# A one-layer perceiver kernel: first group's queries and keys in two token parts, other load order, layer norm in 10 steps, new instruction orders

## The chip, the core and the metric

One core of a Trainium2 chip runs the whole layer. TensorE (PE) multiplies and transposes, VectorE (DVE), ScalarE (ACT) and GpSimd (POOL) do the elementwise work, and the queues of SyncE (SP) and ScalarE issue the DMAs. The metric is the device time of one execution in microseconds; the value of a kernel is the median of its runs.

## The reference, cut to what matters

The input is `x`, 64 batches of 32 rows of 256 channels, and a context of 257 rows of 192 channels for each batch. All tensors are float32.

```
x = x + xattn(ln(x), ctx)   # 16 heads of 64; keys, values from the 257 context rows; mask; softmax
x = x + attn(ln(x))         # 16 heads of 16 over the batch's own 32 rows
x = x + ffn(ln(x))          # r * (relu(k)^2 @ W_v), x mixed with its previous row by mu_r, mu_k
ln(x) = (x - mean) / sqrt(var + 1e-5)
```

Each of the first two blocks applies a second layer norm with its own gamma and beta, so one fused scale serves both norms of a block.

## The kernel before, in words

**Tiling.** The 64 batches go in 8 groups of 8 batches (`GB = 8`), a group being 256 token rows (two tiles of 128). Three stages of different groups run at once: the pre stage of group g+1 (norm, transposed input `xnT`, queries `qT`, and keys folded into the queries), the attention of the 8 batches of group g, and the post stage of group g-1 (output product, second attention, gated layer). Keys are never formed: a query times its key weights (`nwk`, `nwkt`) gives a 192 wide row for each head and query, and that row is multiplied with the raw context. Each such number is held as an upper and a lower part of the reduced float type, `qk_h` and `qk_l` for channels 0 to 127 and `qk_t` for both parts of channels 128 to 191. ACT copies the upper part out of PSUM, DVE subtracts it from PSUM for the lower one.

**Jobs and orders.** Every engine but SP runs a list of named jobs, written out by hand for the first, the middle and the last group (`PE_FIRST`, `PE_ORDER`, `PE_LAST` and the same for ACT, DVE and POOL). An engine runs its jobs strictly in that order; semaphores hold a job until what it needs is done. The names, with j the batch in the group:

- `CT:j` transposes the context of batch j on PE (L724), copies it (ACT L1043) and splits it (DVE L1290). `CU:j` and `CL:j` make the upper and lower parts of the untransposed context (ACT L1077, DVE L421 and L422). After `CL:j` nothing reads the loaded buffer `cx_in` of that batch again.
- `S0:j` to `S3:j`: scores of four heads each, five products (PE L780), mask and maximum (DVE L1299), exponent (ACT L1051). `R` is the reciprocal, `N` the normalisation (POOL L564).
- `P0:j`, `P1:j`: transposed probabilities (PE L791, ACT L1059), `U` and `L` their parts (ACT L1070, POOL L430). `AC:j`: probabilities times context (PE L806 to L812), copied by ACT L1083, L1084 and DVE L1312.
- `XT`, `Q0` to `Q3`: transposed norm and queries. `K0` to `K11`: the twelve halves of the six key products (PE L701 and L710, issued by the even ones; ACT L1029 and L1034, DVE L1276 and L1281). In the first group the same jobs are called `H0` to `H11`, and `Q2`, `Q3` are `G2`, `G3`.
- `A`, `B`, `C` followed by a number: one step each of the three layer norms (DVE L1235 to L1258). A step waits for the step before it.
- `LV0`, `LV1`: value product of the last context row of all 64 batches (PE L744, L745, ACT L1175). `F0` to `F2` transpose the gated layer's weights. `OT`, `WO`, `T2`, `QT`, `KT`, `VR`, `SC`, `PT`, `PV`, `T4`, `PJ`, `T3`, `FR`, `FK`, `FV`: post stage. `LT` spreads the last row's probabilities. `Z` is a filler product on PE (L945).
- In the last group the post stage runs in two halves of 128 rows, `.0` and `.1`.

**Start.** PE runs 36 warm-up products (`WARM`), the input transposes, the eight weight transposes of the keys (`WK0` to `WK3`, L984, L985), the last context rows, and queries `Q0` and `Q1` for all 256 rows, each query product being 4 pairs of 256 columns. Only then the list `PE_FIRST` begins.

**SP's queue.** SP issues the loads in program order: input, key weights, first half of the query weights, context 0, second half, contexts 1 to 3, the rest. Then, for group 0, it waits for the copies of `LV0` and `LV1`, issues 16 small DMAs that spread the last row's values (`spread_last_values`, L499), and only then enters the loop over the batches: wait until `AC:j` is done (`ac_done`), load the context of batch j+4 into the same slot (L451, L453). There are four slots.

Of the kernel before, what the change touches and what calls it, by code (L numbers as in the profile page):

```python
# [12 lines left out]
ALU = mybir.AluOpType  # L13
ACT = mybir.ActivationFunctionType
AX = mybir.AxisListType
# [23 lines left out]
RSQRT_SEED = float(0x5F3759DF)  # L39
NEWTON = 3  # L40
# [5 lines left out]
FIRST_USE_0 = {0: 4, 1: 6, 2: 10, 3: 12}  # L46
# [21 lines left out]
    "AC:5 P1:6 K4 P0:7 K6 AC:6 LT P1:7 K8 K10 CT:0 AC:7").split()  # L68
PE_ORDER = (
# [3 lines left out]
    "S1:7 S2:7 FR P0:6 S3:7 FK AC:5 FV P1:6 K0 K2 AC:6 P0:7 K4 LT P1:7 K6 CT:0 K8 K10 AC:7").split()  # L73
PE_LAST = (
# [5 lines left out]
    "T3.1 Z16 FR.0 FK.0 FR.1 FK.1 Z17 Z18 FV.0 Z19 FV.1").split()  # L80
ACT_FIRST = (
# [4 lines left out]
    "U0:6 K3 P1:6 K4 U1:6 AC:5 K5 K6 CU:7 P0:7 K7 AC:6 U0:7 P1:7 K8 U1:7 K9 CT:0 K10 K11 AC:7").split()  # L86
ACT_ORDER = (
# [4 lines left out]
    "AC:5 P1:6 U1:6 K0 K1 K2 K3 AC:6 P0:7 K4 U0:7 K5 K6 K7 P1:7 CT:0 U1:7 K8 K9 K10 K11 AC:7").split()  # L92
ACT_LAST = (
# [5 lines left out]
    "T3.0 M0.0 T3.1 M0.1 FK.0 EZ.0 FK.1 EZ.1").split()  # L99
# [1410 lines left out]
```

## Time and profile before

| | |
|---|---|
| median of 3 runs | 874.78 us (873.36 to 875.11) |
| profiled execution | 873.3 us |
| its span, first to last instruction | 870.3 us |
| mean granted TensorE clock | 0.988 |
| PE busy | 812.6 us, 93% |
| DVE, ACT, POOL busy | 611.1, 600.3, 423.7 us |
| 16 DMA engines, queue of SP | 12.3% of the span |

The profiled execution took 3.0 us more than its span. The granted clock is a mean of two levels: 1.0 is 2.4 GHz, 0.5 is 1.2 GHz. In the 40 slices of the page PE stands at 98 to 99% nearly everywhere in the middle (digits of 9, and 8 at the borders of the groups), and lower in the first five slices, which are 109 us, and in the last five.

### The profile page before, as it was taken

The page shows a single profiled execution, that of the slowest core. Times are in us where ns is not written, and L with a number is a line of the kernel's source. Part 1 is how long each engine was busy: PE and PEld are TensorE (multiplying, and loading weights), DVE is VectorE, ACT ScalarE, POOL GpSimd, SP SyncE. Part 2 cuts the span into 40 slices and gives each one's busy share as a digit, 9 for nine tenths or more (in the row PEclk, how much of TensorE's full clock was granted, in tenths as well). Part 3 has the DMA queues.
Part 4 walks back from the last instruction along what each step waited for, and adds up shares of the span by engine and source line. Part 5 has one row for each costly group of instructions (what it writes and reads, how often), then busy time and mean ns, then how long its engine had stood idle before and what let it go on. Part 6 is the DMA issues. An engine that isn't in the chain of part 4 may idle for free.

```text
span 870.3 us, 20253 instructions
## 1 busy us (share of the span) xinstructions
PE 812.6 (93%) x7355; PEld 669.2 (77%) x7355; DVE 611.1 (70%) x1871; ACT 600.3 (69%) x1423; POOL 423.7 (49%) x664
## 2 busy tenths in 40 slices
PE   8779999999999989999999989999999989888886
PEld 7568669896788858896788868896788857677664
DVE  4744575879577884879567884879668874767375
ACT  2659876798477875799567975799567875667422
POOL 1155524665437534766337533766337534656211
PEclk9899999999999999999999999999999999999999
DMA  8311010010101020011101120110100110010000
GB/s 236 109 25 37 26 50 13 25 26 26 50 26 26 25 62 13 26 27 25 50 18 29 29 62 14 26 26 25 50 14 26 36 51 10 17 26 1 26 2 12
DMA packets 49521, 30.50 MB, mean 35 GB/s; under 512 B 22928, under 2 KB 48336, under 8 KB 49424
## 3 DMA queue, kind: packets, MB, share of 16 engines
q1 hardware_dynamic: 48528, 29.12, 12.3%
q8 instruction: 59, 0.97, 0.4%
q14 instruction: 38, 0.31, 0.1%
q10 hardware_dynamic: 896, 0.10, 0.1%
HBM read 26.85 MB, written 2.10 MB: 33 GB/s over the span
## 4 chain that ended last, share of the span: by engine, by line
PE 74%; DVE 12%; ACT 8%; issue 4%; SPq 1%; POOL 1%; DMA 0%; POOLq 0%; ACTq 0%; DVEq 0%
PE score L780 16%; PE pre L665 6%; PE post L866 6%; PE probT L791 5%; DVE qk_t L1281 4%; PE post L875 3%; PE aux L724 3%; PE ac_main L806 3%; PE ac_tail L808 2%; PE ac_main L807 2%; PE ac_tail L812 2%; PE ac_main L811 2%; DVE qk_l L1276 2%; PE post L846 2%; PE post L884 2%
## 5 line engine op out<-in xcount | busy, mean ns | idle before, releaser
L430 POOL TENSOR_TENSOR prT_l<-prT,prT_h 128x512 fp32r<-128x512 f32 x128 | 164.5, 1290 | 173.0 <-ACT prT_h L1070 172.8
L564 POOL TENSOR_SCALAR pr<-pr,rsum,poison 128x257 f32<-128x257 f32 x256 | 148.8, 593 | 138.0 <-DVE rsum L1305 137.0
L1299 DVE CUSTOM_DVE_ANT_0 sm<-score,mbias 128x257 f32<-128x257 f32 x256 | 106.5, 420 | 92.6 <-PE score L780 78.8
L1051 ACT ACTIVATE pr<-sm,nmx 128x257 f32<-128x257 f32 x256 | 128.8, 505 | 42.9 <-DVE nmx L1299 37.5
L780 PE MATMUL score<-cT_h,qk_h 128*128 128x258 f32 x256 | 91.6, 358 | 6.2 <-DVE qk_t L1281 4.7
L1059 ACT ACTIVATE prT<-probT 128x512 f32<-128x512 f32 x128 | 75.6, 591 | 30.0 <-PE probT L791 28.2
L791 PE MATMUL probT<-ident,pr 128*128 128x128 f32 x512 | 78.8, 277 | 9.3 <-ACT prT L1059 7.0
L1070 ACT ACTIVATE prT_h<-prT 128x512 fp32r<-128x512 f32 x128 | 80.2, 627 | 8.2 <-PE ac_tail L812 7.4
L791 PEld LDWEIGHTS probT<-ident,pr 128*128 128x128 f32 x512 | 60.3, 142 | 19.5 <-issue 7.1
L780 PE MATMUL score<-cT_h,qk_t 128*128 128x258 f32 x256 | 73.7, 288 | 0.0
L780 PE MATMUL score<-cT_h,qk_l 128*128 128x258 f32 x256 | 73.4, 287 | 0.0
L780 PE MATMUL score<-cT_l,qk_h 128*128 128x258 f32 x256 | 73.3, 286 | 0.0
L780 PE MATMUL score<-cT_l,qk_t 128*128 128x258 f32 x256 | 73.1, 286 | 0.0
L780 PEld LDWEIGHTS score<-cT_h,qk_h 128*128 128x128 f32 x256 | 49.3, 192 | 17.7 <-DVE qk_t L1281 7.6
L1083 ACT ACTIVATE act_low<-ac_tail 64x512 f32<-64x512 f32 x64 | 38.1, 595 | 35.3 <-PE ac_tail L812 33.7
L1290 DVE TENSOR_TENSOR cT_l<-aux,cT_h 128x512 fp32r<-128x512 f32 x64 | 43.5, 679 | 24.8 <-ACT cT_h L1043 24.0
L1312 DVE TENSOR_TENSOR act_<-ac_tail,act_low 64x256 f32<-64x256 f32 x128 | 52.9, 413 | 7.9 <-ACT act_low L1083 6.7
L806 PE MATMUL ac_main<-prT_h,c_hl 128*128 128x512 f32 x128 | 55.2, 431 | 2.8 <-ACT prT_h L1070 2.2
L665 PE MATMUL pre<-xnT,wq 128*128 128x256 f32 x232 | 55.6, 382 | 0.0
L780 PEld LDWEIGHTS score<-cT_l,qk_h 128*128 128x128 f32 x256 | 49.7, 194 | 1.4
L866 PE MATMUL post<-wo,qT 128*128 128x256 f32 x224 | 50.6, 379 | 0.0
L808 PE MATMUL ac_tail<-prT_h,c_hl 128*128 128x512 f32 x128 | 50.3, 393 | 0.0
(336 smaller groups left out, 2195.6 us busy)
## 6 DMA issues: line engine op xcount, KB each, us to landing
cx_in<-in_ctx_dram SPq DMA_DIRECT2D x64, 192.0 KB, 2.4
cx_in<-in_ctx_dram SPq DMA_DIRECT2D x64, 64.0 KB, 2.3
xn<-in_x_dram SPq DMA_DIRECT2D x8, 256.0 KB, 3.2
xb<-in_x_dram SPq DMA_DIRECT2D x8, 256.0 KB, 3.3
out_dram<-yo SPq DMA_DIRECT2D x7, 256.0 KB, 3.0
wq<-in_L_xattn_Wq_dram SPq DMA_DIRECT2D x2, 512.0 KB, 7.8
wo<-in_L_xattn_Wo_dram SPq DMA_DIRECT2D x1, 1024.0 KB, 8.2
wqkv<-in_L_attn_W_qkv_dram SPq DMA_DIRECT2D x1, 768.0 KB, 8.7
```

What stands on the lines that cost most here:

```text
L430: eng.tensor_tensor(prT_l[:, :, cut], prT[:, :, cut], prT_h[:, :, cut], ALU.subtract).then_inc(prob_lower, 1)
L564: last = pool.tensor_scalar(p, p, rsum[:, j % 2, t:t + 1], poison[:, 0:1], ALU.mult, ALU.mult)
L665: last = pe.matmul(bank[:, i * TOK:(i + 1) * TOK], wq[:, k, (2 * n + i) * P:(2 * n + i + 1) * P], xnT[:, k, :], start=(k == 0), stop=(k == 1))
L780: last = pe.matmul(score[t % 2][:, 0:NK + 1], q[:, j, tile], c, start=(i == 0), stop=(i == len(products) - 1))
L791: last = pe.transpose(probT[:, m * 256 + i * P:m * 256 + (i + 1) * P], pr[j % 2][:, 2 * half + i, m * P:(m + 1) * P], ident[:])
L806: pe.matmul(ac_main[:], c[:, m, UPPER], prT_h[:, m, :], start=(m == 0), stop=False)
L808: pe.matmul(ac_tail[:], c[:, m, TAILS], prT_h[:, m, :], start=(m == 0), stop=False)
L866: last = pe.matmul(bank[:, 0:DM], qT[:, k, w * P:(w + 1) * P], wo[:, k, :], start=(k == 0), stop=(k == NPAIR - 1))
L1051: act.activation(pr[j % 2][:, t, :], sm[:, t % 2, :], ACT.Exp, bias=nmx[:, j % 2, t:t + 1], scale=-1.0, accum_out=ssum[:, j % 2, t:t + 1]) ...
L1059: act.activation(prT[:, :, half * 256:(half + 1) * 256], probT[:].rearrange("p (m c) -> p m c", m=2), ACT.Copy).then_inc(probT_copied, 1)
L1070: act.activation(prT_h[:, :, cut], prT[:, :, cut], ACT.Copy).then_inc(prob_upper, 1)
L1299: dve.tensor_tensor_reduce(sm[:, t % 2, :], score[t % 2][:, 0:NK], mbias[:], DH ** -0.5, BIG, ALU.add, ALU.min, nmx[:, j % 2, t:t + 1]).th ...
```

## The change

The edits are these.

1. **First group in two token parts.** The queries of group 0 are computed as `D0`, `D1` (rows 0 to 127, that is batches 0 to 3; heads 0 to 7, then 8 to 15) and `G0`, `G1` (rows 128 to 255). Each is 8 products of 128 columns. The keys become `H0` to `H5` for the first part and `I0` to `I5` for the second, each pair of them covering two of the six key products at 128 columns. Copies and splits follow, with half as many columns. The scores of batch 0 now wait for `H` alone (`S0` for two of six, `S1` for four, the rest for six), those of batch 4 for `I`.
2. **Query weights are loaded ahead of the key weights** on SP's queue, and the start of PE is `WARM`, `XT`, then the list, which begins with fillers `O` and `D0`; the key weights' transposes are `J0` to `J3` in the list. Last rows (`LF`), constants (`CN`) and context 0 (`T0`) are list jobs as well.
3. **Context loads** wait for `c_lower` (the split `CL:j`) where they waited for `ac_done` (the product `AC:j`). The 16 small DMAs move from ahead of the batch loop to behind the load that batch 1 triggers.
4. **Layer norm** has 10 steps (16 instructions for 256 rows) where it had 12 (19): one step makes the seed of the reciprocal root, and two refinements with other constants take the place of three.
5. **New orders** for all four engines and all three lists. `Z` has 19 fillers where it had 20.

```diff
 sp.dma_start(xn[:], token_rows(x_rows, 0)).then_inc(x_in, 16)
+sp.dma_start(wq[:, :, 0:512], wq_columns[:, :, 0:512]).then_inc(wq_in, 16)
 sp.dma_start(wk_main, Wkv[0:P, 0:NH * DH]).then_inc(wk_staged, 16)
 sp.dma_start(wk_tail, Wkv[P:DC, 0:NH * DH]).then_inc(wk_staged, 16)
-sp.dma_start(wq[:, :, 0:512], wq_columns[:, :, 0:512]).then_inc(wq_in, 16)
 load_ctx(0, 0)
...
-                else:
-                    spread_last_values()
                 for j in range(GB if has_pre else GB - NCTX):
-                    sp.wait_ge(ac_done, g * GB + j + 1)
+                    sp.wait_ge(c_lower, g * GB + j + 1)
                     load_ctx(g * GB + j + NCTX, j % NCTX)
+                    if g == 0 and j == 1:
+                        spread_last_values()
...
+            def first_queries(name):
+                half, tokens = int(name[1]), slice(0, TP) if name[0] == "D" else slice(TP, TOK)
...
+                pe.wait_ge(pre_free, nth_pre({"G0": "D0", "G1": "G0"}.get(name, "XT"), 0))
+                for i in range(4):
+                    pair = 4 * half + i
+                    for k in range(2):
+                        last = pe.matmul(FIRST_PRE_BANKS[name][:, i * TP:(i + 1) * TP], wq[:, k, pair * P:(pair + 1) * P],
+                                         xnT[:, k, tokens], start=(k == 0), stop=(k == 1))
...
                 elif stage == 2:
                     dve.tensor_scalar(w[:, own], mv[:, n, own, 1], -0.5 * scale, -0.5 * shift, ALU.mult, ALU.add)
-                    last = dve.tensor_scalar(lw[:, n, 3, own], mv[:, n, own, 1], scale, shift, ALU.mult, ALU.add)
+                    last = dve.tensor_scalar(w2[:, own], mv[:, n, own, 1], -1.6875 * scale, -1.6875 * shift, ALU.mult, ALU.add)
                 elif stage == 3:
-                    last = dve.tensor_scalar(li[:, n, own], lw[:, n, 3, own].bitcast(I32), 1, None, ALU.logical_shift_right)
-                elif stage == 4:
-                    last = dve.tensor_scalar(y[:, own].bitcast(I32), li[:, n, own], -1.0, RSQRT_SEED, ALU.mult, ALU.add)
+                    last = dve.tensor_scalar(y[:, own].bitcast(I32), w[:, own].bitcast(I32), -0.5, RSQRT_SEED, ALU.mult, ALU.add)
```

The new list of PE for the first group, up to the fourth batch, and the tail of a middle group before and after:

```
PE_FIRST  O0 O1 O2 O3 O4 O5 D0 J0 O6 J1 J2 H0 J3 LF T0 D1 G0 H2 H4 CT:1 O7 O8 O9 S0:0 S1:0 I0 G1 S2:0 S3:0 I2
          S0:1 CT:2 S1:1 P0:0 S2:1 S3:1 I4 P1:0 S0:2 S1:2 P0:1 CT:3 S2:2 S3:2 AC:0 P1:1 S0:3 S1:3 CT:4 S2:3 LV0
          P0:2 S3:3 LV1 P1:2 S0:4 F0 AC:1 P0:3 S1:4 F1 CT:5 S2:4 S3:4 XT F2 AC:2 P1:3 S0:5 S1:5 Q0 S2:5 P0:4 CT:6
before    K0 K2 AC:6 P0:7 K4 LT P1:7 K6 CT:0 K8 K10 AC:7 | S0:0 CT:1 S1:0 OT0 S2:0 S3:0 OT1
after     K0 K2 P0:7 AC:6 K4 K6 P1:7 LT K8 AC:7 CT:0 K10 | S0:0 CT:1 S1:0 OT0 CT:2 S2:0 S3:0 OT1
```

In DVE's last list the steps `C0.0` to `C8.0` stand ahead of `PJ.1` now (before: `C0.0` to `C2.0`), and `C9.0`, the step that writes the normed half, stands behind `C2.1`. `FV.0` moves ahead of `SG.1`.

## Rows read from the trace of the kernel before

**Rows 1.** Windows: stretch, length, busy PE, PEld, DVE, ACT, POOL, clock, DMA.

```profile
8.42:118.86 110.44, 94.43 (x651) 75.04 (x650) 60.49 (x190) 78.41 (x181) 43.21 (x77) 0.94 0.26 74
...
30.00:35.50 5.50, 2.05 (x25) 1.26 (x21) 4.29 (x12) 4.96 (x11) 1.11 (x3) 0.89 0.00 0
35.50:43.00 7.50, 7.46 (x32) 6.20 (x32) 5.02 (x19) 3.48 (x10) 1.33 (x4) 0.62 0.01 3
...
68.00:98.00 30.00, 29.23 (x191) 26.44 (x190) 13.66 (x54) 26.85 (x66) 17.86 (x27) 1.00 0.14 36
98.00:117.40 19.40, 16.20 (x147) 10.70 (x146) 14.64 (x32) 17.40 (x35) 10.48 (x17) 1.00 0.11 28
117.40:711.00 593.60, 579.13 (x5341) 480.86 (x5341) 451.55 (x1372) 444.23 (x1049) 317.32 (x486) 1.00 0.11 30
```

**Rows 2.** PE's waits, 120 to 720 us: total, times, longest.

```profile
PE score L710 <- DVE qk_l L1276: 4.3, 6, 0.7
...
PE probT L791 <- ACT prT L1059: 2.7, 6, 0.5
```

**Rows 3.** Timeline, 47 to 62 us: SP's queue and the PE transpose behind it.

```profile
49.44 9.08 SPq L499 DMA_DIRECT2D lvc<-kM  x14
...
58.56 0.44 SPq L451 DMA_DIRECT2D cx_in<-in_ctx_dram  x1
...
61.49 0.97 PE L724 MATMUL aux<-ident,cx_in 128*128 128x128 f32 x4 [4.88 <-DMA cx_in<-in_ctx_dram]
```

**Rows 4.** Timeline of PE: first scores of batch 4 and of group 1.

```profile
68.25 0.36 PE L780 MATMUL score<-cT_h,qk_h 128*128 128x258 f32 x1 [0.20 <-issue]
...
118.86 0.36 PE L780 MATMUL score<-cT_h,qk_h 128*128 128x258 f32 x1 [0.78 <-DVE qk_t L1281]
```

**Rows 5.** The chain that ended last: start, duration, what.

```profile
1.53 6.89 PE score L989 x36
...
21.02 1.02 PE score L701 x16
...
65.76 0.23 PE ac_main L806
...
75.21 1.73 PE pre L665 x8
76.94 0.44 PE probT L791 x4
...
84.92 0.60 PE score L780 x5
...
820.60 0.60 PE score L852 x16
...
825.15 0.89 PE post L875 x8
```

**Rows 6.** ACT and DVE by shape: busy us, mean ns, idle before.

```profile
L1121 ACT ACTIVATE qT<-score 128x256 f32<-128x256 f32 x2 | 0.7, 381 | 2.6 <-PE score L858 2.6
...
L1029 ACT ACTIVATE qk_h<-score 128x512 fp32r<-128x512 f32 x30 | 17.1, 595 | 1.1 <-PE score L701 1.1
...
L1312 DVE TENSOR_TENSOR act_<-ac_tail,act_low 64x256 f32<-64x256 f32 x128 | 52.9, 413 | 7.9 <-ACT act_low L1083 6.7
```

**Rows 7.** The page: DMA issues; KB each, median us to landing.

```profile
wq<-in_L_xattn_Wq_dram SPq DMA_DIRECT2D x2, 512.0 KB, 7.8
```

**Rows 8.** Timeline, 311 to 316 us, around a group's border.

```profile
311.54 2.41 ACT L1034 ACTIVATE qk_t<-score 64x512 fp32r<-64x512 f32 x4
...
312.91 2.81 DVE L1281 TENSOR_TENSOR qk_t<-score,qk_t 64x512 fp32r<-64x512 f32 x4
...
315.78 0.39 PE L780 MATMUL score<-cT_h,qk_h 128*128 128x258 f32 x1 [0.65 <-DVE qk_t L1281]
```

**Rows 9.** Timeline of the end, 851 to 856 us.

```profile
851.95 0.42 DVE L1390 TENSOR_TENSOR x<-ac_tail,xb 128x256 f32<-128x256 f32 x1 [3.38 <-PE ac_tail L915]
...
855.51 0.41 PE L637 MATMUL pre<-ident,hn 128*128 128x128 f32 x2 [2.73 <-DVE hn L1249]
```

More of the change, by code:

```diff
@@ L336, in nth, with nth_pre @@
             return g * len(jobs) + list(jobs).index(name) + 1
+        def nth_pre(name, g):
+            if g == 0:
+                return PRE_FIRST.index(name) + 1
+            return len(PRE_FIRST) + nth(PRE, name, g - 1)
         def stream(orders):
@@ new lines, in key_products @@
+                last = [None, None]
+                for i in range(2):
+                    for e in range(2):
+                        cols = slice(place + i * n_tok, place + (i + 1) * n_tok)
+                        for c in range(2):
+                            rows, cut = slice(e * 64, e * 64 + 64), slice(c * 64, c * 64 + 64)
+                            if kind == "main":
+                                pair, weight = 2 * at + i, nwk[rows, 2 * at + i, cut]
+                            else:
+                                pair, weight = 4 * at + 2 * i + c, nwkt[rows, 4 * at + 2 * i + c, :]
+                            last[e] = pe.matmul(banks[e][cut, cols], weight, qT[rows, pair, tokens], start=True, stop=True)
@@ new lines, in key_products, with first_key_job @@
+                return last
+            def first_key_job(name):
+                n, later = int(name[1:]), name[0] == "I"
+                if n % 2:
+                    return
+                job = n // 2
+                pe.wait_ge(pre_free, nth_pre(f"{'DG'[later]}{min(job, 1)}", 0))
+                if name == "H0":
+                    pe.wait_ge(setup_copied, 2)
+                if name == "H2":
+                    pe.wait_ge(setup_copied, 4)
+                    pe.wait_ge(left_split, 1)
+                if name in ("H4", "I0"):
+                    pe.wait_ge(qk_split, 2 if name == "H4" else 4)
+                if name in ("I2", "I4"):
+                    pe.wait_ge(qk_split, 6 if name == "I2" else 10)
+                banks = FIRST_QK_BANKS[later * len(FIRST_QK) + job]
+                for x, d in enumerate(FIRST_QK[job]):
+                    last = key_products(d, banks, slice(TP, TOK) if later else slice(0, TP), x * TOK, TP)
+                for e in range(2):
+                    last[e].then_inc(qk_full, 1)
@@ L941, in post_job, with key_weights, last_rows, warm @@
                 last.then_inc(post_full, 1)
+            def key_weights(n):
+                if n == 0:
+                    pe.wait_ge(wk_staged, 32)
+                if n == 3:
+                    pe.wait_ge(setup_copied, 1)
+                for i in range(2):
+                    pair = slice((2 * n + i) * P, (2 * n + i + 1) * P)
+                    pe.transpose(wk_bank[n][:, i * DC:i * DC + P], wk_main[:, pair], ident[:])
+                    last = pe.transpose(wk_bank[n][:, i * DC + P:(i + 1) * DC], wk_tail[:, pair], ident[0:64, 0:64])
+                last.then_inc(keys_full, 1)
+            def last_rows():
+                pe.wait_ge(left_staged, 32)
+                pe.wait_ge(setup_copied, 2)
+                pe.transpose(left_bank[:, 0:NB], left_in[:, 0:P], ident[0:NB, 0:NB])
+                pe.transpose(left_bank[:, NB:2 * NB], left_in[:, P:256], ident[0:NB, 0:NB]).then_inc(left_full, 1)
+            def warm():
+                pe.matmul(warm_bank[:, 0:P], ident[:], ident[:], start=True, stop=True)
             def keep_clock():
@@ L1019, in pre_job, with first_queries @@
                 last.then_inc(pre_free, 1)
+            def first_queries(name):
+                act.wait_ge(pre_full, nth_pre(name, 0))
+                half, tokens = int(name[1]), slice(0, TP) if name[0] == "D" else slice(TP, TOK)
+                act.activation(qT[:, 4 * half:4 * half + 4, tokens], FIRST_PRE_BANKS[name][:].rearrange("p (n t) -> p n t", n=4),
+                               ACT.Copy).then_inc(pre_free, 1)
             def qk_copy(n, g):
@@ L1156, in post_job, with last_rows @@
                 last.then_inc(post_copied["ScalarE"], 1)
+            def last_rows():
+                act.wait_ge(left_full, 1)
+                rows_in = left_bank[:, 0:2 * NB]
+                by_group = rows_in.rearrange("p (k g b) -> p k g b", k=2, g=NG)
+                act.wait_ge(zeroed, 1)
+                act.activation(left[:, 0].rearrange("p (b g) -> p g b", g=NG), by_group[:, 0], ACT.Copy)
+                for r in range(2):
+                    rows = slice(r * 64, r * 64 + 64)
+                    act.activation(left[rows, 1 + r].rearrange("p (b g) -> p g b", g=NG), by_group[rows, 1], ACT.Copy)
+                act.activation(left_h[:].rearrange("p k b -> p (k b)"), rows_in, ACT.Copy).then_inc(left_upper, 1)
             def run():
                 for name, g, j in stream(ACT_STREAM):
-                    if name[0] == "H":
-                        qk_copy(int(name[1:]), 0)
-                    elif name in ("G2", "G3"):
-                        pre_job("Q" + name[1], 0)
+                    if name in KEYS_FIRST:
+                        first_key_copy(name)
+                    elif name in PRE_FIRST and g == 0 and name != "XT":
+                        first_queries(name)
+                    elif name == "T0":
+                        context(0, "CT0", 0)
+                    elif name == "LF":
+                        last_rows()
                     elif name == "CT":
@@ L1227, in layer_norm @@
                 before = 0 if half == 1 else g * LN_LINKS
-                w, y, q = lw[:, n, 0], lw[:, n, 1], lw[:, n, 2]
+                w, y, q, w2 = (lw[:, n, i] for i in range(4))
                 if stage > 0:
@@ L1271, in qk_lower, with first_key_lower @@
                 d, e = divmod(n, 2)
+                key_lower(d, e, qk_banks[d % 2][e][:], slice(0, GB)).then_inc(qk_split, 1)
+            def first_key_lower(name):
+                n, later = int(name[1:]), name[0] == "I"
+                dve.wait_ge(qk_upper, later * N_FIRST_QK + n + 1)
+                job, e = divmod(n, 2)
+                bank = FIRST_QK_BANKS[later * len(FIRST_QK) + job][e]
+                for x, d in enumerate(FIRST_QK[job]):
+                    last = key_lower(d, e, bank[:, x * TOK:(x + 1) * TOK], slice(HB, GB) if later else slice(0, HB))
+                last.then_inc(qk_split, 1)
```

300 lines of the change are left out of this document (138 added, 162 removed), and 78 rows, old and new, of tables (ACT_FIRST, ACT_LAST, ACT_ORDER, DVE_FIRST).

## The prediction

> **What bounds the kernel now.** I began with the page's shares and its 40 slices: PE is busy 93% of the span, no other engine over 70%, and PE's clock is at its upper level almost throughout. So the end is set by PE's work and by the gaps in it, and the question for every edit is which gap of PE it closes. The windows show where the gaps are [rows 1]. From 117.4 to 711 us PE is busy 579.13 of 593.60 us at clock 1.00; the 14.5 us of idle there are four waits in each of six group borders, 14.0 us in all and 2.33 us a group; the largest (4.3 us) and the smallest (2.7) of the four stand in [rows 2]. In the opening, from the end of the warm-up to the first score of group 1, 8.42 to 118.86 us, PE is busy 94.43 of 110.44 us at clock 0.94: 16.0 us idle, and since a clock of 0.94 is the mean of 1.0 and 0.5, 0.06 x 110.44 = 6.6 us more lost to work at 1.2 GHz. With neither, the same work is 110.4 - 16.0 - 6.6 = 87.8 us. Third, the waits and the timeline name the largest single gap: PE stands 4.88 us before the context transpose of batch 4, because its load stands in SP's queue behind the 16 small DMAs, fourteen of which take 9.08 us [rows 3]. Another gap is 30 to 35.5 us, where PE is busy 2.05 of 5.5 us, waiting for copies and splits of keys, and behind it the clock is 0.62 for 7.5 us, which costs 0.38 x 7.5 = 2.9 us [rows 1].
>
> **Context loads and the 16 DMAs.** The load for batch 4 now waits for the split of batch 0's context, which stands ahead of batch 0's second score on DVE, and the small DMAs are behind the load for batch 5. The 4.88 us go. What is late next is batch 6's load: it stands behind the 16 DMAs, and these behind the copy of `LV1`. They take 16 x 9.08 / 14 = 10.4 us, copy and landing add 0.6 and 61.49 - 58.56 = 2.9 us, so batch 6 is there 13.9 us after `LV1`'s product. In that time PE has, by the list up to `CT:6`, 7 score tiles, 8 jobs of four transposes (P, XT, CT:5, F0 to F2), 1 query job and 2 of `AC`: 7 x 0.60 + 8 x 0.44 + 1.73 + 2 x 10 x 0.23 = 14.1 us [rows 5]. It is covered with 0.2 us to spare; if that cover fails it costs what is missing, and at most the 4.88 us of before. In later groups no context wait is among the four, so the earlier loads give nothing there.
>
> **Query weights first.** Both 512 KB halves take about 7.8 us to land [rows 7], the first issued at 2.4 us. The three transfers that change places carry the same bytes, so the last of the three lands near 10 us in either order. `D0` needs the query weights and the copies of `XT`, which run to 10.0 us; the key weights are needed at 11.9, behind `D0`. Neither waits for the load. The input transposes cannot start before the warm-up ends at 8.42 [rows 5], so the 0.6 us that the shorter first norm gives is hidden there: nothing.
>
> **Two token parts, and the new opening.** The columns are the same, the instructions twice as many. A query job of 128 columns costs between 8 x 0.111 us by the post row of 128 columns (825.15 us, 0.89 for 8) and its share by columns, 1.73 / 16 = 0.108: 64 of them are 6.9 to 7.1 us for 6.9 before. For keys the nearest row is the 64x64 product of 128 columns, 16 in 0.60 us, 37.5 ns each; 192 of them are 7.2 us for 6 x 1.02 = 6.1 before [rows 5]. So PE gains 1.1 to 1.3 us of work; the bounds are 0 (columns alone) and 6.1 (an instruction costs as at 256 columns); I take 1.3. ACT and DVE pay too: half the columns cost 0.38 for 0.60 us, and a 64x256 operation 0.41 [rows 6]; twelve copies of 8 x 0.60 + 8 x 0.60 = 9.6 us become 16 x 0.38 + 16 x 0.38 = 12.2 at worst and, as neighbouring ones overlap, some 1.5 us more than before. DVE likewise gains 2.5. What it buys is the order of things. Walked by the new list with these prices, PE gets `D0` 10.1 to 11.9, the key weights and `H0` to 17.1, `D1`, `G0`, `H2`, `H4` to 23.1, the first score at 24.2; `I0` and `G1` lie between scores; `AC:0` runs 39.4 to 41.7, and batch 4's first score, with both `LV` done, comes at 49.3. In the trace that score is at 68.25 [rows 4], with `AC:1` and `XT` done as well (2.7 us) and `P1:2` not (0.44): like for like 66.0 against 49.3, 16.7 us.
>
> That walk has every engine ready at once. Two things say not to take it whole. ACT: it has 78.4 us of work in the stretch and gets 1.5 more, so in a stretch of 94 us it would be busy 85%, and between 68 and 98 us it already runs at 26.85 of 30 [rows 1]; its list is what holds `AC:0`, `P0:1` and the keys `I`. And the 3.2 us of idle in 98 to 117.4 us come from the key jobs at the group's end, which keep their form. So I give 87.8 + 1.3 + 8.4 of gaps = 97.5 us for the stretch, 12.9 less. The 8.4 is 3.2 for the end, 2.0 for `D0`'s wait and the fillers `O7` to `O9`, and 3.2 that ACT or a short low clock takes. Bounds: 17 by the walk, 5 if only batch 4's wait goes.
>
> The Trainium skill speaks against this part. Its page "TensorE: Matmul & The Clock Gate", section "Back-to-back issue gap", says that a stream of weight load and product pairs runs at about 81 ns a product at 128 columns and not at the column time. By it 192 key products would be 15.6 us, 9.5 more than now, and the gain would be 4 us. The trace has the same form, 64x64 with 128 columns, at 37.5 ns, four in flight on different quarters of the array [rows 5]; so I go by the row.
>
> **Layer norm.** Three instructions of 19 go for 256 rows. In the middle DVE is busy 451.55 of 593.60 us, and its norm steps fill gaps between PE's scores: nothing. In the end it counts: the second projected half's sum starts at 851.95 and PE waits 2.73 us until the first half's norm is written and transposed at 855.51 [rows 9]. With steps `C0.0` to `C8.0` ahead of that sum, in a time in which DVE is idle 3.38 us, the first half needs only the sum, three short steps and the write behind it: 0.42 + 0.45 + 0.2 + 0.2 + 0.4 = 1.8 us, so the transpose comes at 853.8, 1.7 earlier. The second half is 1.0 earlier, two steps of 0.2 and less interleaving. `FV.0` ahead of `SG.1` is neutral: the last store hangs on `FV.1`. I take 1.5 from this and 0.5 from the second half's earlier norm, two steps shorter with PE behind it: 2.0, bounds 0 and 4.
>
> **Orders of the middle groups.** Here the gain or loss is six times a small number. The new tail puts `CT:0` and `AC:7` between `K8` and `K10`. Before, `S0:0` waits 0.65 us for the second key split of `K8`/`K9`, ACT's four copies of 2.41 us and DVE's four of 2.81 starting 1.2 and 2.6 us after `K8` [rows 8]. After, PE has 10 x 0.23 + 0.44 + 1.02 = 3.8 us from `K8`'s end to `S0:0`, 0.44 more cover, but the copy of `CT:0` stands behind the four on ACT and its split of 0.69 behind them on DVE, which makes `S0:0` ready 0.7 us later. `K8` itself has lost `CT:0` as cover and ACT's `U0:7` ahead of it. Counting from `K0` to `S0:0` I get 15.1 us in both orders. The other two waits keep their form. I take 0, bounds -7 (half of the 14.0 gone) and +6 (1 us a group). The last group's reordering, 4 us around it either way by its own idle, I take at 0.
>
> **Sum.** The profiled execution: 873.3 - 12.9 - 2.0 = 858.4. The median of the runs is 874.78, 1.5 above it, so 858.4 to 859.9: I say 859.
>
> **The rivals.**
> - *ACT bounds the opening.* For it: 26.85 of 30 us busy in 68 to 98 us. Against: 80 us of work in 97.5. If it must run its whole list at 89.5% behind its idle until 15.6 us (the first key copy): 80 - 4 = 76 us of work at 0.895 is 85 us, to 100.6, and the key tail adds 8 us more than PE's floor: the gain is 6 to 8, time 866.
> - *The orders help the middle.* For it: all 14.0 us are the same four waits. Against: my count. Half of them gone: 852.
> - *The block of 16 DMAs only moves.* If `CT:6` waits as `CT:4` did, 4.88 us, and the clock stays: 864. Against: 14.1 us of PE work over 13.9.
> - *A product of 128 columns costs as one of 256.* Against: 37.5 and 111 ns beside 64 and 216 [rows 5], in this very program. For it: those rows are 24 products in the calm end. Keys would cost 6.1 us more than before and queries 6.9, 13.0 in place of 1.3: 871. The page on TensorE named above has keys dearer still.
> - *Slower: group borders.* `S0:0` waits for `CT:0`'s split, last in a queue of four key splits. Priced above at +0.7 against +0.44 of cover. If more stood ahead of it, each border would lose; the gain of 15 is used up at 15 / 7 = 2.1 us a border, seven of them. And after 3.45 us of idle in 5.5 the clock was low long enough to cost 2.9 [rows 1]: 2.1 + 2.9 a border make 859 + 35 = 894; without the clock 874 to 876. The page "TensorE: Matmul & The Clock Gate" of the Trainium skill, section "HAM oscillation — how this bites in real kernels", has gaps bring the clock down each time, with half of the work's speed as the price.
>
> **How the numbers follow.** Forecast 0.61 at 859 (own range 854 to 864), ACT 0.15 at 866, orders 0.10 at 852, the 16 DMAs 0.06 at 864, products at 256 columns' price 0.02 at 871, slower border 0.06 at 876 and up. A measurement of this kernel can tell 0.2%, 1.7 us, from no change. The first five cases are faster, 0.94 together; from them I take 0.01 for what I have not seen. Of the last case, with that, 0.05 is slower and 0.02 the same: 0.93, 0.02, 0.05. The range from 850 to 868 takes in the first four with their own spread.
>
> **What would show it.** Right: `CT:4` without a DMA wait, and that load issued near 25 us; the first score of batch 4 near 50 to 53 us, of group 1 near 106; clock 0.98 or more from 8.4 to 106; 192 key products of the first group under 45 ns apart; 99 us a group as before; the `T3.0` transpose 1.5 us or more nearer to `PJ.1`'s sum. Wrong: key or query products at 80 ns; a border wait over 2 us; ACT without a gap from 40 to 100 us and PE waiting for it; a wait before `CT:6`.

## The result and the profile after

The changed kernel takes 844.56 us (median of 4 runs, 844.47 to 844.77), the kernel before beside it 874.94 us (873.36 to 876.49): a ratio of 0.966, 95% interval 0.9641 to 0.9679. It is 30.4 us faster. The forecast was 859 us with a range of 850 to 868: the direction was right, the gain half of what came, and the time is outside the range.

The first score of each group divides the span (profiled executions, us; "a group" is the mean of the six periods of groups 1 to 6):

| kernel | first score | from it to group 1's | a group | last group | span | execution |
|---|---|---|---|---|---|---|
| before | 28.25 | 90.61 | 98.60 | 159.87 | 870.3 | 873.3 |
| after | 23.75 | 75.76 | 98.46 | 152.44 | 842.7 | 844.6 |
| forecast, against before | -4 | -9 | 0 | -2 | -15 | |
| measured | -4.5 | -14.9 | -0.1 each, -0.8 | -7.4 | -27.6 | -28.7 |

The last 1.1 us lie outside the span (3.0 before, 1.9 after).

Now the page and the windows of the kernel after (stretch, length, busy PE, PEld, DVE, ACT, POOL, clock, DMA), which answer to [rows 1]:

```profile
PE 799.9 (95%) x7501; PEld 665.1 (79%) x7501; DVE 600.3 (71%) x1813; ACT 604.0 (72%) x1439; POOL 415.0 (49%) x664
PEclk9999999999999999999999999999999999999999
```

```profile
8.42:99.51 91.09, 88.65 (x795) 75.20 (x795) 64.02 (x203) 77.64 (x196) 43.44 (x77) 1.00 0.34 96
50.00:70.00 20.00, 20.00 (x135) 18.30 (x134) 10.87 (x39) 18.38 (x48) 12.37 (x20) 1.00 0.22 54
70.00:90.00 20.00, 19.26 (x155) 15.28 (x154) 12.18 (x33) 18.51 (x44) 13.04 (x24) 1.00 0.11 27
90.00:99.51 9.51, 7.95 (x61) 5.92 (x62) 9.09 (x19) 8.36 (x16) 4.11 (x5) 1.00 0.31 84
99.51:690.26 590.75, 575.85 (x5339) 477.81 (x5338) 440.60 (x1316) 446.78 (x1045) 310.68 (x484) 1.00 0.11 30
690.26:842.70 152.44, 128.55 (x1331) 105.18 (x1329) 92.37 (x280) 78.12 (x197) 58.07 (x89) 1.00 0.05 13
```

From 8.42 us to the first score of group 1 PE is busy 88.65 of 91.09 us, where before it was 94.43 of 110.44 at clock 0.94. The clock never falls there. And ACT is busy 36.89 of the 40 us from 50 to 90, 92%, while PE is busy 39.26 of them: a full ACT beside a full PE. PE's waits of that stretch (total, times, longest; the first is the wait at the very start) are all that is left of its idle time, 1.2 + 0.6 + 0.6 = 2.4 us:

```profile
PE score L993 <- POOL ident L532: 1.5, 1, 1.5
PE ac_main L835 <- DVE act_ L1387: 1.2, 1, 1.2
PE score L712 <- DVE qk_l L1352: 0.6, 1, 0.6
PE pre L712 <- DVE qk_t L1356: 0.6, 1, 0.6
```

SP's timeline answers to [rows 3], and PE's to [rows 4] and [rows 5]: the load for batch 4 is issued at 24.57 us and its transposes start at 43.05 with no wait; the 16 DMAs take 10.62 us behind batch 5's load; the first keys' products, which the program places on four quarters of the array, overlap.

```profile
24.57 0.38 SPq L452 DMA_DIRECT2D cx_in<-in_ctx_dram  x1
46.67 0.37 SPq L452 DMA_DIRECT2D cx_in<-in_ctx_dram  x1
49.87 10.62 SPq L500 DMA_DIRECT2D lvc<-kM  x16
60.53 0.45 SPq L452 DMA_DIRECT2D cx_in<-in_ctx_dram  x1
```

```profile
9.68 2.02 PE L673 MATMUL probT<-xnT,wq 128*128 128x128 f32 x16
14.79 0.28 PE L712 MATMUL pre<-qT,nwk 64*64 64x128 f32 x2
14.90 0.28 PE L712 MATMUL pre<-qT,nwk 64*64 64x128 f32 x2
43.05 0.60 PE L746 MATMUL aux<-ident,cx_in 128*128 128x128 f32 x4
49.56 0.37 PE L807 MATMUL score<-cT_h,qk_h 128*128 128x258 f32 x1
99.51 0.28 PE L807 MATMUL score<-cT_h,qk_h 128*128 128x258 f32 x1
```

In 0.11 us between two such rows PE issues four key products, two of `pre` and two of `post`: 27 ns each. With the step from one job to the next the 192 key products of the first group take 6.05 us, 31 ns each; before, 96 of twice the columns took 6.1. In the last group the output projection's first product and, at the end, the two rows that answer to [rows 9]:

```profile
786.71 3.69 PE L895 MATMUL pre<-wo,qT 128*128 128x256 f32 x16 [0.17 <-ACT qT L1179]
827.23 0.42 DVE L1465 TENSOR_TENSOR x<-ac_tail,xb 128x256 f32<-128x256 f32 x1 [3.56 <-PE ac_tail L944]
829.05 0.41 PE L638 MATMUL pre<-ident,hn 128*128 128x128 f32 x2 [0.99 <-DVE hn L1308]
```

From the second half's sum to the first half's transpose it is 1.82 us, against 3.56 before. Behind it stand four products for each half, `FR.0` and `FR.1`. The same program ("after again" below) had them at the other clock level in a second execution; first the kernel after, then that one:

```profile
831.40 1.10 PE L961 MATMUL post<-wrT,kM 128*128 128x256 f32 x4 [0.34 <-DVE kM L1479]
```

```profile
831.10 2.04 PE L961 MATMUL post<-wrT,kM 128*128 128x256 f32 x4 [0.34 <-DVE kM L1479]
```

From `FR.0` to `FR.1` it is 1.83 us in the first, 3.29 in the second and 3.05 in the kernel before. So 1.2 us of the last group's 7.4 are an execution in which the clock stayed up, and not the change.

### The profile page after: what moved, and what is told of

Its sections match the earlier page's. It is cut to its first block, busy times and chain, and to the rows that moved or that the text cites. A ratio compares the mean times of both kernels' runs of the same rounds, so it can differ in the third digit from the quotient of the medians.

```text
span 842.7 us, 20502 instructions
## 1 busy us (share of the span) xinstructions
PE 799.9 (95%) x7501; PEld 665.1 (79%) x7501; DVE 600.3 (71%) x1813; ACT 604.0 (72%) x1439; POOL 415.0 (49%) x664
## 4 chain that ended last, share of the span: by engine, by line
PE 78%; DVE 14%; ACT 3%; issue 3%; POOL 1%; POOLq 0%; ACTq 0%; DVEq 0%
PE score L807 17%; PE probT L818 6%; PE post L895 6%; PE pre L657 6%; DVE qk_t L1356 4%; DVE qk_l L1352 3%; PE post L904 3%; PE aux L746 3%; PE ac_main L835 3%; PE ac_tail L837 3%; PE ac_main L836 3%; PE ac_tail L841 3%; PE ac_main L840 2%; PE post L875 2%; PE post L881 2%
## 5 line engine op out<-in xcount | busy, mean ns | idle before, releaser
L565 POOL TENSOR_SCALAR pr<-pr,rsum,poison 128x257 f32<-128x257 f32 x256 | 146.3, 582 | 131.2 <-DVE rsum L1380 131.1
L818 PEld LDWEIGHTS probT<-ident,pr 128*128 128x128 f32 x512 | 58.5, 141 | 16.3 <-issue 12.2
L835 PE MATMUL ac_main<-prT_h,c_hl 128*128 128x512 f32 x128 | 55.5, 434 | 4.2 <-ACT prT_h L1128 3.0
L657 PE MATMUL pre<-xnT,wq 128*128 128x256 f32 x224 | 52.9, 379 | 0.0
L1101 ACT ACTIVATE cT_h<-aux 128x512 fp32r<-128x512 f32 x64 | 37.8, 590 | 17.8 <-PE aux L746 13.4
L836 PE MATMUL ac_main<-prT_h,c_hl 128*128 128x512 f32 x128 | 50.1, 392 | 0.0
```

The costliest lines, as they stand in the source:

```text
L565: last = pool.tensor_scalar(p, p, rsum[:, j % 2, t:t + 1], poison[:, 0:1], ALU.mult, ALU.mult)
L657: last = pe.matmul(pre[:, i * TOK:(i + 1) * TOK], wq[:, k, (2 * n + i) * P:(2 * n + i + 1) * P], xnT[:, k, :], start=(k == 0), stop=(k == 1))
L818: last = pe.transpose(probT[:, m * 256 + i * P:m * 256 + (i + 1) * P], pr[j % 2][:, 2 * half + i, m * P:(m + 1) * P], ident[:])
L835: pe.matmul(ac_main[:], c[:, m, UPPER], prT_h[:, m, :], start=(m == 0), stop=False)
```

## The experiments

Fifteen other kernels ran, and the kernel after again. The last column is the median of the kernel before on the same chip (single runs of it 869.2 to 875.8 us, the longer ones with a lower mean clock, 0.984 to 0.994); the split by first scores tells more than the medians:

| kernel | first score | to group 1's | a group | last group | median us | before beside it |
|---|---|---|---|---|---|---|
| b_sp | 29.48 | 88.22 | 98.58 | 160.1 | 869.3 | 871.7 |
| b_rest | 29.05 | 90.78 | 98.45 | 154.06 | 865.9 | 871.7 |
| b_ln10 | 28.00 | 90.49 | 98.93 | 158.25 | 873.7 | 872.7 |
| after again | 23.50 | 75.75 | 98.45 | 153.97 | 845.5 | 873.9 |
| a_acdone | 23.43 | 84.12 | 98.46 | 152.52 | 852.2 | 871.7 |
| a_spread0 | 24.45 | 86.93 | 98.45 | 154.22 | 858.0 | 871.7 |
| a_wkfirst | 24.55 | 75.78 | 98.43 | 152.49 | 845.0 | 872.7 |
| a_nofill | 23.57 | 76.24 | 98.46 | 152.55 | 844.6 | 873.9 |
| a_actload | 23.42 | 76.80 | 98.41 | 152.44 | 846.1 | 873.9 |
| a_oldorder | 24.42 | 75.77 | 98.56 | 154.63 | 846.7 | 871.3 |
| a_oldlast | 23.68 | 75.81 | 98.36 | 159.67 | 851.2 | 871.3 |
| a_cbehind | 24.02 | 75.77 | 98.44 | 155.27 | 847.6 | 871.3 |
| a_ln12 | 24.07 | 75.82 | 99.24 | 158.65 | 855.9 | 871.3 |
| a_openonly | 24.05 | 75.80 | 98.58 | 158.88 | 852.7 | 872.7 |
| a_v1 | 24.19 | 75.77 | 98.43 | 151.84 | 844.3 | 873.9 |
| a_v2 | 23.44 | 75.80 | 98.43 | 150.76 | 843.1 | 872.7 |

The first score varies by 1.0 us between kernels with one opening, with the start of XT's transposes (7.42 to 8.50 us), for which PE waits on the norm or is still at the warm-up; from there to the first score it is 15.9 to 16.0 us in all of them. The last group varies by 1.5 us between two executions of one kernel ("after again" against after), by whether the clock falls in the last 20 us. The other two columns repeat to 0.1 us between these two. A name with a is an edit of the kernel after, with b of the kernel before.

**The context loads alone (b_sp).**

```
-                else:
-                    spread_last_values()
                 for j in range(GB if has_pre else GB - NCTX):
...
-                    sp.wait_ge(ac_done, g * GB + j + 1)
+                    sp.wait_ge(c_lower, g * GB + j + 1)
                     load_ctx(g * GB + j + NCTX, j % NCTX)
+                    if g == 0 and j == 1:
+                        spread_last_values()
```

> The kernel before with the context loads' change alone: SyncE waits for the copies (c_lower) and the 16 copies of last rows stand behind batch 1's load. Theory (TensorE is starved in the opening by whatever it waits for, and ScalarE does not hold it): TensorE's 4.88 us wait for batch 4's context goes, and with it the lower clock behind it; first score of group 1 from 118.86 to 112 to 114 us, the time 868 to 870 us against 874.9. Rival (ScalarE bounds the opening, so what TensorE gains it waits off again at ScalarE): at most 2.5 us, 872.4 or more. Second rival (the block of 16 only moves and holds batch 6): the same, with a wait of TensorE for a context load near 70 us.

The ratio is 0.9984 (0.9963 to 1.0005): it cannot be told from no change. The median lies in the theory's 868 to 870 us, but the kernel before took 871.7 beside it and not 874.9, and the first score of group 1 came at 117.70 us and not at 112 to 114: the theory failed. The stretch got 2.4 us shorter, though the DMA's 4.9 us of wait are gone. PE's waits from 28 to 118 us:

```profile
PE probT L791 <- ACT prT L1059: 3.0, 3, 1.2
PE ac_main L806 <- DVE act_ L1312: 1.9, 1, 1.9
PE post L701 <- DVE qk_l L1276: 1.9, 1, 1.9
PE probT L791 <- POOL pr L564: 1.6, 1, 1.6
PE post L701 <- DVE qk_t L1281: 0.9, 1, 0.9
```

No DMA is among them. Before, the first was 2.5 us and the second was not there; the last stands there too, just ahead of 28 us. So 4.9 us went and 2.4 came: in the old opening another chain stood right behind the DMA's. The rival's size, 2.5 us at most, is right. That ScalarE alone sets it is not shown: 0.5 us of the new wait are its own, but 1.9 are for a VectorE step, which stands in VectorE's list behind one that had waited 2.06 us for an exponent of ScalarE. The clock from 50 to 70 us was 0.91, as before.

**Parts of that edit taken back in the new opening (a_acdone, a_spread0).**

```
 a_acdone
-                    sp.wait_ge(c_lower, g * GB + j + 1)
+                    sp.wait_ge(ac_done if g == 0 else c_lower, g * GB + j + 1)
 a_spread0
-                    if g == 0 and j == 1:
+                    if g == 0 and j == 0:
```

> The kernel after, but the context loads of the first group wait for the products with the probabilities (ac_done) again; the 16 copies stay behind batch 1's load. Theory (in this opening every stall of TensorE counts in full): context 4 lands near 44.9 where its transposes want it at 43.05, context 5 is late by another 1, context 6 behind the 16 copies by 2, context 7 by 1 to 2: plus 4 to 7 us, 849 to 852. Rival (the slack of the opening takes the stalls up): plus at most 2 us.

> The kernel after with the 16 copies of last rows ahead of context 5's load, not behind it. Theory: they are issued from 49.9 to 60.5 us, context 5 lands near 63.8 and TensorE wanted it at 54.47: a stall of 9.3 us, with the lower clock behind it 9 to 11 us in all: 854 to 856. Rival (later slack takes part of it back): plus 5 us or less.

The stretch grows by 8.4 and 11.2 us. PE's waits for context loads, of a_acdone and then of a_spread0, and then two windows, of a_acdone behind its waits and of a_spread0 around the stall:

```profile
PE aux L746 <- DMA cx_in<-in_ctx_dram: 6.1, 4, 2.2
```

```profile
PE aux L746 <- DMA cx_in<-in_ctx_dram: 8.7, 1, 8.7
```

```profile
70.00:90.00 20.00, 18.80 (x113) 16.33 (x115) 7.62 (x30) 15.83 (x42) 9.39 (x16) 0.92 0.11 29
```

```profile
50.00:70.00 20.00, 11.30 (x63) 10.43 (x63) 4.76 (x20) 9.03 (x23) 6.38 (x13) 0.74 0.16 40
```

Each costs its stall and 2.3 or 2.5 us on top, and the clock, 1.00 there in the kernel after, is 0.92 and 0.74 in these windows: part of the work ran at the lower of the two levels. Slack takes nothing back, and both cost a little more than their theories said (4 to 7 and 9 to 11 us). The edits are not the same as b_sp's: b_sp makes both changes, in every group, and gains 2.4 us in the old opening, while a_acdone takes back only the one, in the first group, and loses 8.4 in the new one. So the smaller part is worth more in the new opening than both in the old, and the two parts of the opening cannot be priced apart and added.

**Everything but the opening (b_rest), and the opening alone (a_openonly).** b_rest has the lists `*_FIRST`, the one-part queries and keys, and the loads of group 0 of the kernel before, with the norm and the other lists of the kernel after; a_openonly the reverse.

> The kernel after with the opening of the kernel before (its first-group orders, all tokens in one part, key weights loaded first, 16 copies first, loads of the first group behind ac_done), but with the new layer norm and the new orders of groups 1 to 7. Theory: the opening is worth 19.35 us by itself and the rest 8 to 9: first score of group 1 near 118.5, end behind the first score of group 7 near 152.5 us, the time 863 to 866 us. Rival (the opening's gain comes partly from the new middle orders or the norm): first score of group 1 below 117 us.

> The kernel after with its opening alone: orders of groups 1 to 7 and the norm of 12 steps as in the kernel before. Theory (norm and orders pay only together; the old orders have room for 12 steps): first score of group 1 as in the kernel after, 75.8 us behind the first score, six periods of 98.6, the last group 159.9: 852.5 to 854.0 us, that is faster than the norm of 12 steps in the new orders (855.9). Rival (the two are independent: the norm costs 11 us wherever it stands, the old orders 8): 860 or more.

Both hold: 90.78 us to group 1, as before's 90.61, with all else new, and 75.80 with all else old. The opening is worth 20.1 us of the 28 to 30 (852.7 against 872.7), the rest 5.8 by b_rest's medians (865.9 against 871.7), less than the 8 to 9 expected; in b_rest's trace the clock fell at the end as in "after again", which is 1.5 us of it.

**Does ACT bound the opening (a_actload)?** Behind each half's upper parts of batches 2 to 7:

```
+                        if g == 0 and j >= 2:
...
+                            act.activation(yo[:]...[:, slot:slot + P], ident[:], ACT.Copy)
```

> The kernel after with twelve more ScalarE copies of 128x128 in the opening (one behind each half's upper parts of batches 2 to 7, into a tile that is free then), 3.3 to 3.7 us of ScalarE's time. ScalarE was busy 36.89 of the 40 us from 50 to 90. Theory (TensorE's queue sets this opening and ScalarE has slack behind each product): first score of group 1 later by 1.5 us at most. Rival (ScalarE bounds the opening): later by 3 us or more.

The twelve copies of 0.30 us, 3.6 us, cost 1.05 us, under the theory's 1.5. ACT now runs 37.86 of the 40 us from 50 to 90, 95%, and PE still 39.21:

```profile
50.00:70.00 20.00, 19.76 (x132) 17.89 (x131) 10.87 (x39) 18.78 (x52) 11.97 (x20) 1.00 0.22 54
70.00:90.00 20.00, 19.45 (x156) 15.40 (x154) 11.70 (x32) 19.08 (x47) 13.14 (x24) 1.00 0.11 27
```

**Fillers (a_nofill) and the weights' place (a_wkfirst).** The first drops `O0` to `O9` from `PE_FIRST`; the second issues the two key-weight loads ahead of `wq`.

> The kernel after without the ten fillers O0 to O9 on TensorE in the opening. Theory (they stand in waits and keep the clock up; the waits themselves do not change): minus 0.2 to plus 0.3 us if the clock stays at its higher level without them, plus 1 to 3 us in the stretch to the first score of batch 0 if it does not. Rival (they cost what they take, 10 products of 128 columns at 0.22 us): minus 1 to minus 2 us.

> The kernel after with the key weights' two loads issued ahead of the first query weights'. Theory (D0 starts at 9.68 us when the norm's transposes are copied; the query weights behind the key weights landed at about 9 to 10 us in the kernel before): first score later by 0 to 0.7 us, the time within 1 us of the kernel after. Rival (the first queries are bound by their weights): plus 1.5 us or more.

Counted from XT's transposes, which lie up to 0.8 us apart in these three executions, the kernel after has `D0` at 1.87 us, the first score at 15.94 and group 1 at 91.70. Without fillers it is 1.87, 15.00 and 91.24: they don't hold `D0` up, cost 0.9 us up to the first score, and half of that is taken back up to group 1; the clock stays at 1.00 without them. From the start of XT's transposes to group 1 PE is busy 87.38 of 91.24 us without the fillers and 89.26 of 91.70 with them, so they are 1.9 us of its busy time. With the key weights first it is 1.86, 15.94 and 91.72: nothing, as predicted.

**The norm and the orders.** a_ln12 takes back the norm of 12 steps, steps 10 and 11 right behind each 9; a_oldorder and a_oldlast take back the `*_ORDER` or `*_LAST` lists without steps 10 and 11; a_cbehind one list:

```
-  PJ.0 C0.0 C1.0 C2.0 C3.0 C4.0 C5.0 C6.0 C7.0 C8.0 PJ.1 C0.1 C1.1 C2.1 C9.0
+  PJ.0 C0.0 C1.0 C2.0 PJ.1 C0.1 C1.1 C2.1 C3.0 C4.0 C3.1 C5.0 C6.0 C4.1 C7.0 C5.1 C8.0 C6.1 C9.0
```

> The kernel after with the last group's four orders of the kernel before (steps 10 and 11 of the norm taken out of them, 20 fillers). Theory (the last group gained 5 us by its order, WO.0 from 101.45 to 96.45 us behind the group's first score, and 1.7 by the norm steps ahead of the other half's projection, and 1.2 by the clock behind it): from the first score of group 7 to the end 158.5 to 159.5 us against 152.4, the time 850.5 to 851.7. Rival (it is the norm's shorter chain that gained): 155.5 or less, plus 3 at most.

> The kernel after with the middle groups' orders of the kernel before (steps 10 and 11 taken out). Theory: six periods of 98.6 in place of 98.4, plus 0.8 to 1.2 us: 845.4 to 845.8. Rival (the new middle orders feed the last group or take up the opening's debts at the border): plus 3 or more, at the first score of group 1 or behind that of group 7.

> The kernel after with one order changed: in VectorE's last group the norm steps C3.0 to C8.0 stand behind PJ.1 and between those of half 1, as in the kernel before. Theory: T3.0 comes 1.0 to 1.5 us later and FR.1 with it, and if TensorE's clock falls before FR.0 another 1.2 to 1.7: plus 1.0 to 3.0 us, 845.6 to 847.6. Rival (the chain of half 1 ends last whatever half 0 does): plus 0.3 or less.

> The kernel after with the layer norm of the kernel before in 12 steps (three Newton steps and a shift), steps 10 and 11 right behind step 9 in every order. Theory: 0.45 us at the start (the first transposes wait for the norm), 0.4 at B9.1 and 0.4 at C9.1 in the last group, nothing in the middle groups: plus 1.0 to 1.5 us, 845.6 to 846.1. Rival (two more links at each of 16 norms delay TensorE at the borders too): plus 2.5 or more; rival (hidden everywhere): 0.3 or less.

> The kernel before with the norm of 10 steps alone. Theory (in the old orders the norm's end is waited for only at the start and, half 0, once at the end): 0.45 us at the start and 0 to 0.5 at the end, ratio 0.9985 to 1.000. Rival (independent of the orders): ratio 0.990 or less, 8 us or more.

a_oldorder loses 0.6 us in the six middle groups, as its theory says. Its median is 0.9 above the range, with two runs of 845.5 us and two of 848: the traced one, one of the slower two, has 154.63 us in the last group, where `FR.1` starts 3.3 us behind `FR.0`, so the clock fell as in "after again".

The last two are the surprise. In the old kernel the short norm gains 1.6 us in the last group (0.5 of it between `FR.0` and `FR.1`, so by the clock), loses 0.3 a group before it, and the ratio is 1.0017 (1.0002 to 1.0032). What costs the 0.3 is not shown. In the new orders the long one costs 11 us, 4.7 in the six middle groups and 6.2 in the last. Of the 6.2, 3.7 lie ahead of `WO.0`, and 1.4 between `FR.0` and `FR.1`, by the clock. PE's waits from 110 to 690 us show the middle groups; the first fence is a_ln12, and in the kernel after, the second, waits of this line are not among those of 1 us or more:

```profile
PE post L640 <- DVE hn L1312: 3.7, 12, 0.5
```

```profile
PE score L807 <- DVE qk_t L1356: 5.0, 5, 1.0
PE pre L712 <- DVE qk_t L1356: 2.7, 6, 0.5
PE score L712 <- DVE qk_l L1352: 2.4, 6, 0.4
PE ac_main L835 <- ACT prT_h L1128: 2.0, 6, 0.3
```

Twelve waits of 0.3 us on average, `T2` and `T3` of six groups: the new lists call for the norms' output as soon as a norm of 10 steps can have it. The old lists do not, and b_ln10 shows that they could not use the shorter norm. Both old (a_openonly, 852.7 us) is faster than the long norm in the new orders (855.9).

In a_oldlast the output projection `WO.0` starts at 792.01 us, 102.38 behind the group's first score, for 96.45 in the kernel after and 101.45 before; the clock falls at the end as well. Its last group is 7.2 us longer than in the kernel after and 5.7 longer than in "after again". In a_cbehind the second sum starts at 827.33 us and `T3.0` 3.11 us behind it, for 1.82 in the kernel after, and the clock from 824.17 us on is 0.86:

```profile
830.44 0.41 PE L638 MATMUL pre<-ident,hn 128*128 128x128 f32 x2 [2.28 <-DVE hn L1308]
832.79 2.04 PE L961 MATMUL post<-wrT,kM 128*128 128x256 f32 x4 [1.17 <-DVE kM L1479]
```

The four products of 832.79 take 2.04 us there, 1.10 at the upper clock. Of the 2.8 us that this order costs against the kernel after, 1.3 remain against "after again", whose clock fell too.

**The end laid out anew (a_v1, a_v2).** From `WO.1` on the end is one chain through the second half, and the first half's steps stand in its way on VectorE. PE's and ScalarE's last lists are moved to match.

```
 a_v2, VectorE
-  B6.1 SC.0 B7.1 B8.1 B9.1 VR.0 SM.0 KM.1 SC.1 VR.1 SM.1     ... C8.0 PJ.1 C0.1 C1.1 C2.1 C9.0 ... FR.0 FR.1 SG.0
+  B6.1 B7.1 B8.1 B9.1 SC.0 VR.0 KM.1 SM.0 SC.1 SM.1 VR.1     ... C8.0 C9.0 PJ.1 C0.1 C1.1 C2.1 ... FR.0 SG.0 FR.1
```

a_v1 has `VR.0 SM.0 KM.1 VR.1 SC.1 SM.1` and keeps the order of `SG.0`.

> The kernel after with four orders of the last group's end changed: SC.0 behind B9.1 on VectorE, three fillers less ahead of T2.1, VR.1 ahead of PT.0 on TensorE and ahead of SC.1 on VectorE, C9.0 ahead of PJ.1 and T3.0 with it. Theory (from WO.1 on the end is one chain through half 1, and half 0 stands in its way on VectorE three times): T2.1 1.0 to 1.3 us earlier, SM.1 another 0.4 to 0.6, the last two stages 0.2 to 0.4: minus 1.5 to 2.2 us, 842.3 to 843.0. Rival (half 0, now later, ends last): minus 0.5 or less.

> The kernel after with the last group's end laid out anew: as a_v1, but SM.0 behind KM.1 (so that GpSimd's W.0 doesn't lie beside KM.1), VR.1's copies behind SM.1, SC.1 ahead of PT.0, PT.1 ahead of PJ.0, SG.0 ahead of FR.1. Theory: KM.1 back at 2.36 us for its two products (3.25 in a_v1), SM.1's end 1.7 us earlier than in a_v1, the last sigmoid 0.4 earlier: minus 1.8 to 2.6 us against the kernel after's 844.5 to 845.5, 842.3 to 843.2. Rival (half 0, now 3 us later, takes over the chain's end): no better than a_v1's 844.3.

a_v1 gained 0.6 us of the last group, less than expected: `T2.1` came 1.2 us earlier, but `KM.1`, two products from SBUF, took 3.25 us, 2.36 before, where GpSimd's product of `W.0` lay beside it. The rows of VectorE and of GpSimd in a_v1:

```profile
812.19 3.25 DVE L1425 TENSOR_TENSOR wq<-xnT,headm 128x1024 f32<-128x1024 f32 x2
```

```profile
812.17 1.05 POOL L595 TENSOR_TENSOR sc<-sc,rs 128x512 f32<-128x512 f32 x1 [6.09 <-DVE rs L1452]
```

In a_v2, with `W.0` behind it, it is 2.36 again, and the last group 1.7 us shorter than in the kernel after:

```profile
811.47 2.36 DVE L1425 TENSOR_TENSOR wq<-xnT,headm 128x1024 f32<-128x1024 f32 x2 [1.32 <-ACT xnT L1195]
```

a_v2 has the lowest median, 843.12 us (842.85 to 844.28). By ratio it cannot be told from the kernel after: 0.9671 (0.965 to 0.9691) against 0.966 and 0.9681 in that one's two sets of runs. Its five spans are 840.5 to 841.6 us; the kernel after's were 842.3 to 843.9 on two chips. The two were not timed side by side; that a_v2 is some 1.5 us faster is what the spans and the last group say.

## Why the prediction was wrong

**The walk was right, the discount on it was not.** Forecast and trace: `D0` from 10.1 and 9.68, first score 24.2 and 23.75, `AC:0` 39.4 and 39.12, batch 4's first score 49.3 and 49.56, load near 25 and at 24.57, the 16 DMAs 10.4 and 10.62 us. The step that failed is "87.8 + 1.3 + 8.4 of gaps = 97.5 us for the stretch". The stretch took 91.09. PE was busy 88.65 us against 89.1 for floor and extra work, but that these are near each other is chance: 1.9 of the 88.65 are the fillers. The work itself was 86.8 us, so the extra 1.3 was not there and the floor was 1.0 lower than I had it. The gaps were 2.4 us of idle, 4.3 with the fillers, and not 8.4. Of the three parts the end's 3.2 was 1.6 (9.51 - 7.95), `D0`'s wait and the fillers' 2.0 were the 1.9 of fillers and no idle time, and ACT with a low clock, 3.2, was 0.9, with the clock at 1.00. So 4.1 us of the miss are the gaps and 2.3 the work. This is 6.4 of the 14.4 us that the forecast missed; the last group is 5.4, the middle 0.8, the time outside the span 1.1 and the step from the profiled execution to the median 0.6. I had set the walk aside because ACT would be 85% busy. It was 85% over the stretch, and 92% from 50 to 90 us. At 95%, in a_actload, TensorE lost a third of what ScalarE was given. An average share does not price a wait.

The walk's own bound of 17 us was too low as well: the first score of group 1 came 19.35 us earlier. The walk ended at batch 4, like for like 66.0 us against 49.56, 16.4. The other 2.9 came behind it, where I had taken the old course over: PE was idle 4.56 us from there to group 1 before and 2.30 after. Small slips did no harm. The cover of batch 6's load holds nine jobs of four transposes, not eight, so 0.6 us and not 0.2, and its transposes started at 63.75 us, 3.2 behind the load's issue, without a wait. In the rival on ACT 15.6 + 85 + 8 is 108.6, which is 10.3 us ahead of 118.86 and not 6 to 8.

**The old opening was a set of chains.** The bound of 5 us "if only batch 4's wait goes" was too high: in the old opening the new loads and the moved block gave 2.4. In the new opening taking back the loads' wait alone costs 8.4. What the split and the new first orders are worth apart from one another was not tried.

**Two terms that are one.** "In the middle ... its norm steps fill gaps: nothing" and "the last group's reordering I take at 0" priced the norm in the old orders and the orders with the old norm. For the norm alone this was near (b_ln10: 1.6 us at the end, 2.0 forecast, though 2.0 were lost in the middle groups). For both together the last group gained 7.4, and 5.0 of it lie ahead of `WO.0`, where neither gives much alone: from the group's first score to `WO.0` it is 101.45 us before, 100.94 with the short norm alone (b_ln10), 100.11 with the new orders and the long norm (a_ln12), and 96.45 with both. Behind it the forecast mechanism came true: from the second sum to `T3.0` 1.74 us less, 1.7 forecast. That this fits so well is in part luck, since the terms written down add up to 1.67 and not 1.8, and the trace has 0.15 more, from the end of the write to the transpose. The 1.2 us less from `FR.0` to `FR.1` are luck altogether: "after again", the same program, does not have them. With its ratio, 0.9681 (0.9656 to 0.9705), the time would still be below 850. The bounds of 4 us on the last group's order were too narrow: a_oldlast is 7.2 us longer there than the kernel after, and 5.7 longer than "after again", where the clock fell too.

**What held.** Middle groups at 0: -0.8 us together. Query weights first: nothing. 128-column products at their columns' price: the keys 27 ns apart within a job, 31 with the steps between jobs, under my 37.5, and 6.05 us in all. The Trainium skill, page "TensorE: Matmul & The Clock Gate", section "Back-to-back issue gap", gives 81 ns a product at 128 columns. By that rule they would be 15.6 us; for 64x64 products on four quarters the trace does not agree. The first norm is 0.59 us shorter, from landed input to `xn` 3.64 us for 4.23; whether the warm-up hides it differs between executions. XT's transposes came 0.45 us earlier in the kernel after, 0.41 behind `xn`, with warm-up products up to their start; in "after again" they came at 7.49 us, 0.06 behind `xn` and waiting for it; in a_nofill at 8.57, 1.15 behind it. Of the rivals, "ACT bounds the opening" is refuted for the new opening; "the block of 16 only moves" also, though a_spread0 shows that one place earlier it costs 11.2 us; the slower border did not come, 98.46 us a group.

## What to carry to other kernels

Discount a walk through a queue's list only by waits that you can name: here the walk hit its marks within 0.5 us and the unnamed discount was the miss. Follow it to the end of the stretch, too; the last 50 us, not walked, gave another 2.9. An edit that frees an engine for a moment is worth what the rest of the stretch can follow: price it in the schedule in which it will run, and a shorter chain together with the order that calls for its result earlier. In this full stretch an idle of 8.7 us cost 11.2, and four that add up to 6.1 cost 8.4. And compare two versions by their first scores before their medians: 1.2 to 1.5 us at this kernel's end come and go with the clock.

## What the runs showed of the hardware

A VectorE product with both inputs in SBUF took 2.11 us beside a GpSimd product of 1.05 us that began 0.02 us ahead of it (a_v1), and 1.22 alone; the GpSimd product took 1.05 us either way. The Trainium skill, page "SBUF — State Buffer", section "SBUF: two separate sides", calls the pair of ports that the two share an "exclusive lock" and "not a bandwidth split". The 0.89 us lost are nearly GpSimd's whole instruction, so the runs agree.

The kernel after's last group took 152.44 or 153.97 us in two executions, with PE's clock 0.99 from 824 us on in the one and 0.84 in the other. PE is busy 11.41 of 18.70 us there in the first, in short pieces. Up to `FR.0`, 141.1 us behind the group's first score, the two are alike to 0.02 us; from `FR.0` to `FR.1` they are 1.83 and 3.29 us. So whether the clock falls is not settled by the program alone, and here it cost 1.5 us.
